# A word of its own for each half-precision product of a recurrence

## What is computed

```python
def step(h, xs):
    xzt, xrt, xht = xs
    z = jax.nn.sigmoid(xzt + h @ U_z + vz)
    r = jax.nn.sigmoid(xrt + h @ U_r + vr)
    hh = jnp.tanh(xht + r * h @ U + vh)
    h_new = (1.0 - z) * h + z * hh
    return (h_new, h_new)
```

## Time and profile before

| | us |
|---|---|
| median of 3 runs (2133.19 to 2134.84) | 2133.65 |
| span of the profiled execution | 2133.2 |
| first to last line 510 (the recurrence) | 20.8 to 1053.8 |
| PE busy | 2095.2 |
| DVE busy | 1572.5 |
| ACT busy | 1025.5 |

### The profile page before, as it was taken

One profiled execution on the slowest core, in us unless ns is written; L12 is line 12 of the kernel. 1 busy time (PEld: TensorE's weight loads), 2 busy tenths in 40 slices (PEclk: granted clock), 3 DMA queues, 4 the chain that ended last, 5 costly groups with the idle time before them and its releaser, 6 DMA issues. The chain is left out here.

```text
span 2133.2 us, 82927 instructions
## 1 busy us (share of the span) xinstructions
PE 2095.2 (98%) x32732; PEld 1968.5 (92%) x32732; DVE 1572.5 (74%) x8995; ACT 1025.5 (48%) x3981; POOL 415.7 (19%) x560
## 2 busy tenths in 40 slices
PE   8999999999999999999999999999999999999997
PEld 7899999999999999999768888767999999999997
DVE  6887877787777887787745555593777777777775
ACT  3565565665555565656555776533222222222221
POOL 0000000000000000000000000445455555555553
PEclk6555555555555555555599999999999999999998
DMA  3001000000000000000002322223888888888882
GB/s 127 4 4 44 4 4 4 4 4 4 4 4 4 4 4 4 4 4 4 3 1 92 111 84 80 107 70 133 299 268 276 278 267 276 279 268 277 278 264 58
DMA packets 55558, 213.72 MB, mean 100 GB/s; under 512 B 11578, under 2 KB 40960, under 8 KB 46976
## 3 DMA queue, kind: packets, MB, share of 16 engines
q1 hardware_dynamic: 36276, 184.41, 23.5%
q0 software_dynamic: 17408, 23.61, 5.9%
q10 hardware_dynamic: 1484, 0.40, 0.1%
HBM read 192.82 MB, written 15.57 MB: 98 GB/s over the span
## 5 line engine op out<-in xcount | busy, mean ns | idle before, releaser
L1891 PE MATMUL bank<-xe,ring 128*128 128x160 f32 x3072 | 438.8, 299 | 0.7 <-DVE xe L1949 0.7
L1891 PEld LDWEIGHTS bank<-xe,ring 128*128 128x128 f32 x3072 | 422.7, 190 | 0.9 <-issue 0.9
L1942 DVE STREAM_TRANSPOSE turned<-ye 32x64 f32<-32x64 f32 x1240 | 291.5, 235 | 16.2
L869 PEld LDWEIGHTS bank<-keep_part,Us 128*128 128x128 f16 x6120 | 276.0, 111 | 1.6 <-DVE keep_part L781 0.4
L1659 POOL MEMSET cum<- 128x320 f32 x1 | 0.4, 365 | 1349.7 <-POOLq L1051 1349.7
L869 PE MATMUL bank<-keep_part,Us 128*128 128x4 f16 x6120 | 259.3, 170 | 0.4 <-DVE keep_part L781 0.3
L1927 ACT ACTIVATE gate_f<-bank 128x160 f32<-128x160 f32 x384 | 116.4, 303 | 284.7 <-PE bank L1891 283.7
L869 PE MATMUL bank<-raw,Us 128*128 128x4 f16 x6132 | 241.3, 167 | 0.5 <-DVE raw L805 0.4
L1833 POOL DMA_INDIRECT out_rows<-res,to_row x128 | 192.3, 1503 | 227.2 <-DVE res L1961 193.9
L510 ACT ACTIVATE r_h<-bank 128x8 f32<-128x8 f32 x512 | 92.8, 181 | 278.9 <-PE bank L869 278.4
L1902 PE MATMUL bank<-mid,ring 128*128 128x160 f32 x1536 | 219.1, 299 | 0.0
(11 more groups left out here) (279 smaller groups left out, 4051.4 us busy)
## 6 DMA issues: line engine op xcount, KB each, us to landing
ring<-in_ew SPq DMA_DIRECT2D x64, 2304.0 KB, 9.2
raw<-in_L_cond_ew SPq DMA_DIRECT2D x16, 1024.0 KB, 6.2
ctx_rows<-rows SPq DMA_DIRECT2D x2, 1280.0 KB, 7.0
dense_w<-in_L_ffn_W SPq DMA_DIRECT2D x2, 1024.0 KB, 9.3
dense_w<-in_L_cond_sw SPq DMA_DIRECT2D x2, 1024.0 KB, 6.3
out_rows<-res,to_row POOLq DMA_INDIRECT x128, 4.8
xT<-in_xT SPq DMA_DIRECT2D x2, 864.0 KB, 10.7
dense_w<-in_sw1T SPq DMA_DIRECT2D x1, 1536.0 KB, 11.1
```

The lines of the kernel that those rows point to most:

```text
L869: last = nc.tensor.matmul(pre[g][q][:, jj, m, :], Us[:, g, p, k, m * P:(m + 1) * P], x[part][:, k * B:(k + 1) * B], start=False, stop=Fals ...
L1891: last = nc.tensor.matmul(bank[f % UPS][:, s_ * CAP:(s_ + 1) * CAP], w1[u][:, k, s_ * FFN + f * P:s_ * FFN + (f + 1) * P], xe[e % 2][:, k] ...
L1942: last = nc.vector.transpose(y[:, :, q, :], ye[e % 2][q * SQ:(q + 1) * SQ, :, j * SQ:(j + 1) * SQ])
```

## The change

Each of the tiles `rh_high` and `step_high` gets a fourth dimension of 2, and only the element 0 of it is used: an element of half precision then starts every 4 bytes instead of every 2. The place 2 of the eight groups of three, which lines 768 and 785 write and PE reads, has a stride of 12 bytes, not 6. The scan reads 24 elements at a stride of 4 bytes, not 2. The memsets ahead of the recurrence clear the whole new tiles. `rh_low` and `step_low` keep their layout.

Each of the two tiles grows from 48 to 96 bytes per partition; both tiles of the high products still start at a multiple of 32 bytes. Nothing else moves: the instructions, their order and their semaphores are the same on every engine.

```diff
         r_h, z_cand = t("r_h", [P, C2, 3]), t("z_cand", [P, C2, 3])
-        rh_high, step_high = t("rh_high", [P, C2, 3], F16), t("step_high", [P, C2, 3], F16)
+        rh_words, step_words = t("rh_high", [P, C2, 3, 2], F16), t("step_high", [P, C2, 3, 2], F16)
+        rh_high, step_high = rh_words[:, :, :, 0], step_words[:, :, :, 0]
         rh_low, step_low = t("rh_low", [P, C2, 3], F16), t("step_low", [P, C2, 3], F16)
...
-                for f in (r_h, z_cand, rh_high, step_high, step_low):
+                for f in (r_h, z_cand, rh_words, step_words, step_low):
                     nc.vector.memset(f[:], 0.0).then_inc(s_zero, 1)
...
                     return nc.vector.tensor_tensor_scan(low[:].rearrange("p c s -> p (c s)"), factors[:].rearrange("p c s -> p (c s)"),
-                                                        high[:].rearrange("p c s -> p (c s)"), 0.0, ALU.mult, ALU.subtract)
+                                                        high.rearrange("p c s -> p (c s)"), 0.0, ALU.mult, ALU.subtract)
```

## The result

The changed kernel is 0.3% slower: median 2141.03 us (6 runs, 2140.41 to 2141.85) against 2133.49 of the kernel before (6 runs, 2133.19 to 2135.27); the ratio is 1.0032, 95% interval 1.0021 to 1.0042. The forecast was 2132.6 in a range of 2126 to 2141. The time came out where the slower rival had it, in which the hop is what costs (2140.8), though not by its numbers.

A forecast was written before the change was run, and what follows sets the result against it. The recurrence was taken as bound by a circle of latencies among ACT, DVE and PE. Writes gave -2 ns a step, -1.0 us; scans, products and hidden preamble 0, so 2133.65 became 2132.6 us, range 2126 to 2141.

The forecast's parts named there:

- the slower rival: Lines 768 and 785: elements spread over twice the bytes cost 7 ns more each, +14 ns a step, 2140.8 us; chance 0.19.
- What bounds the recurrence: Recurrence, 512 steps: a circle of latencies through ACT, DVE and PE, 2.00 us a step, each changed write once in it.
- A nanosecond on 768 counts in full, since scan and PE move alike: Rh side: a nanosecond saved on line 768 counts in full, though PE's row is last by about 10 ns.
- A nanosecond counts at all: Recurrence: the writes' -2 ns a step was multiplied by 512 steps to give -1.0 us.
- The price of the write: Lines 768 and 785: new write priced at line 801's 3 ns; 785 changes by 0, 768 by -2 ns.
- The bound of +7 ns: Lines 768 and 785: upper bound if the excess comes a second time, +14 ns a step, +7.2 us.
- What reading costs: DVE's strided inputs: 4 ns for two, so 2 for one, taken off the 7 ns excess of 785 and 768.
- Scans 0, products 0, preamble hidden: Line 630's scans and PE's high products change by 0 ns; memsets' at most 156 ns more hides behind DVE's 7.9 us wait.
- a sign of being wrong: Mechanism wrong if a scan changes by more than 3 ns or the span's last 1079 us change at all.
- The faster rival: Lines 768 and 785: half words at 6 bytes cost the excess; both fall to 167 ns, -14 ns a step, 2126.5; chance 0.15.
- The rule of the Trainium skill that I let the row overrule: DVE writes: full rate needs runs of two adjacent 4-byte words; about 6 ns new on each write, 6 us in all.
- PE's fetch: Slower rival, rh_high and step_high products: 4 ns more each, 44 ns a step, +22.5 us, 2156; chance 0.04.

The follow-up runs named there:

- the shifted tiles: Kernel before with both high tiles' layout (half precision, stride 6 bytes) moved on by 10 bytes; ratio of times 0.9999 (0.9990 to 1.0009), recurrence 1033.3 us.
- The first chain: Kernel before plus single DVE instructions ahead of the recurrence, writing at various strides; half precision 166 ns at 2 bytes, 185 at 12, 195 at 16 and 24.
- the second: Kernel before plus another chain of single instructions, varying start, order, pairs and engine; half-precision writes alternating between two 16-byte pieces took 194 ns.

## Why the prediction was wrong

- *What bounds the recurrence:* right. A circle of latencies, in which the two writes stand; 23 ns more in two instructions lengthened 512 steps by 16 ns each.
- *A nanosecond on 768 counts in full, since scan and PE move alike:* wrong. PE's row of rh_high products does begin 53 to 54 ns behind the write, before and after, but its end hangs on line 838's product, and 10 ns of PE's lateness did not move with DVE. It was to be asked at the earlier trace rows: PE last by 10 ns, with 0.33 us for the eight loads against 0.29 on the step side, has to have a reason. Of the 3.5 us that are missing from 11.8 this product holds back some 2.1 us, an estimate from the records (335 steps that pay 4.6 of 11 ns); the rest falls on steps 28 to 35 of the step side and 36 to 39 of the rh side.
- *A nanosecond counts at all:* also wrong in the small. The sides of a step come in lengths 6.7 ns apart, so the 2 ns that were forecast would not have shown as 1.0 us; the shifted tiles' 2 and 2 ns made 0.4 us and not 2.0.
- *The price of the write:* this is the step that failed and turned the sign. I gave the new write line 801's 3 ns, a single-precision write, and so forecast 0 and -2 ns; measured are 12 and 11. The half-precision write at 12 bytes is 19 ns over a contiguous one and 11 over that at 6. The stride of the nearest row was right and its type was not; its position behind another instruction hid only some 2 ns. The bound of +7 ns, made by doubling today's excess, was too low as well: the excess at 6 bytes is 8 and at 12 bytes 19.
- *What reading costs:* two strided inputs cost 4 ns, as taken; one costs 0 and not 2. Nor was it right to take these off the excess to find the write's share, since read and write do not add up: the 6-byte write alone, with contiguous inputs, is 8 ns over.
- *Scans 0, products 0, preamble hidden:* right in all three. The scans stayed at 208 even with a stride of 8 bytes, rh_high's and step_high's products at 171 and 169 (173 and 168 before), and the preamble's memsets at 78 ns each. That the last stretch changed by 0.8 us, which I had named as a sign of being wrong, is none: untouched, it varies by 4.6 us over the traces.
- *The faster rival*, that half words at 6 bytes are what costs: against it stands that a word of one's own side by side still pays 4 ns and either half of a word the same.
- *The slower rival:* its mechanism is the one that came, at 11 and 12 ns and not 7 each; that its 2140.8 is the measured time is luck: 23 ns a step less what PE's lateness held back came near its 14 ns. The rule of the Trainium skill that I let the row overrule (Vector Engine (DVE) Microarchitecture Reference, section 5.2) had the sign right, and the estimate from it of 6 us in all was nearer than my sum. Its figure for a destination stepping 24 words can't be held against a run here, since the widest stride is 6 words (24 bytes) and the page measured 4-byte elements. There half precision pays 195 - 166 = 29 ns over eight columns, 3.6 ns a column, and single precision 1.0; the page's 2.50 against 1.05 would be 1.5.
- *PE's fetch:* refuted, as expected: the products' medians are 166 and 167 ns at 12 bytes and 168 at 24, against 167 and 166 before.

The SBUF — State Buffer page of the Trainium skill, in "Door 1: The DMA port swizzle", describes 16-byte cachelines and a penalty for each access that crosses to a new one. The first chain agrees in the length, as the price stops rising at 16 bytes, and the second in that alternating between two pieces costs as much as going on to new ones. They do not agree that eight bf16 elements of stride are free: half precision pays 4 ns at a stride of two elements and 19 at six.

## What to carry to other kernels

Do not spread half-precision elements that are written one by one: counted in changes of a 16-byte piece, each was worth some 4 ns to the write of 8 columns, from DVE and from ACT, and padding to whole words does not help. When the price of an access is taken from a neighbour, the neighbour must match in type and not only in stride; if none does, the range has to say so. And where two things end almost together on one side of a loop and not on the other, find out what the later one stands behind before a saved or lost nanosecond is carried through in full. Look, too, whether the lengths of a loop's parts lie on a grid: here a saving under 6.7 ns on one side may give nothing.

## What the runs showed of the hardware

- Half-precision writes of 8 columns from idle on DVE: 166, 170, 174, 178, 185, 195, 195 ns at 2, 4, 6, 8, 12, 16 and 24 bytes; single precision 166, 168, 170, 174 at 4, 8, 12 and 24.
- The same on ACT: 208 contiguous, 228 at 12 bytes, 237 at 16 bytes in half precision; 208 contiguous and 213 at 12 bytes in single.
- Adjacent pairs of half words, pairs 16 bytes apart: 168 ns, where single half words at 8 bytes, with as many changes of piece, take 178.
- A scan's second input in half precision at 2, 4 and 8 bytes: 208 ns for 24 columns each time.
- The two sides of a step of this recurrence have lengths 6.7 ns apart: 987, 993, 1000, 1007, 1013 ns.
